# A macaron block (MoE, windowed top-k attention, MoE) on one core: an extra turn without a search, gates and value copies on ScalarE, two bias adds on GpSimd, a new interleaving

## The reference

```python
x = x + 0.5 * ffn(layernorm(x))      # layer zero
x = x + attn(layernorm(x))
x = x + 0.5 * ffn(layernorm(x))      # layer one, the same weights

def attn(x):                         # in windows of 128 tokens
    q, k, v = x @ Wq.T + bq, x @ Wk.T + bk, x @ Wv.T + bv
    scores = q @ k.T / sqrt(128)
    attn = softmax(scores where among the row's 32 largest, else -inf)
    out = leaky_relu(attn @ v, 0.01)
    return layernorm(out + x) * gamma + beta

def ffn(x):                          # 8 experts of width 384, the best 2 per token
    n = layernorm(x) * ln_gamma + ln_beta
    top_v, top_i = top_k(softmax(n @ router_w.T), 2)
    gates = softmax(top_v)
    return sum over the two of gate * swiglu_e(n) + swiglu_shared(n)
```

## Time and profile before

| | |
|---|---|
| median of 3 runs | 585.45 us (584.99 to 585.77) |
| span of the profiled execution | 581.5 us |
| TensorE busy | 500.6 us, 86% |
| VectorE busy | 388.7 us, 67% |
| GpSimd busy | 332.0 us, 57% |
| ScalarE busy | 330.0 us, 57% |
| mean granted TensorE clock | 0.951 |

### The profile page before, as it was taken

One profiled execution on the slowest core, in us unless ns is written; L12 is line 12 of the kernel. 1 busy time (PEld: TensorE's weight loads), 2 busy tenths in 40 slices (PEclk: granted clock), 3 DMA queues, 4 the chain that ended last, 5 costly groups with the idle time before them and its releaser, 6 DMA issues.

```text
span 581.5 us, 14497 instructions
## 1 busy us (share of the span) xinstructions
PE 500.6 (86%) x3928; PEld 458.6 (79%) x3928; DVE 388.7 (67%) x1688; ACT 330.0 (57%) x792; POOL 332.0 (57%) x491
## 2 busy tenths in 40 slices
PE   2588999989999989999977499996899999799781
PEld 1466999979899989998974369794889989799780
DVE  5558864732558989879887958999785624222574
ACT  3367556565467777667753357673655546555430
POOL 2273766875565675356674405664566765565542
PEclk9989999999999999999977569997999999999996
DMA  6944858766886554766412254431668767676993
GB/s 184 316 112 167 261 188 237 243 233 239 284 260 218 190 187 173 258 226 205 155 47 59 69 195 176 160 112 54 209 224 257 248 221 246 228 262 237 322 320 124
DMA packets 88012, 117.82 MB, mean 203 GB/s; under 512 B 11848, under 2 KB 60880, under 8 KB 87936
## 3 DMA queue, kind: packets, MB, share of 16 engines
q1 hardware_dynamic: 76208, 96.75, 49.8%
q0 software_dynamic: 9312, 19.16, 9.5%
q10 hardware_dynamic: 2416, 0.99, 0.7%
HBM read 26.57 MB, written 26.19 MB: 91 GB/s over the span
## 4 chain that ended last, share of the span: by engine, by line
PE 52%; SPq 15%; ACT 9%; DMA 7%; issue 7%; DVE 5%; POOL 3%; ACTq 1%; POOLq 0%; DVEq 0%
PE ps_y L730 12%; PE ps_g L716 11%; PE ps_u L721 6%; SPq L441 6%; PE ps_h L721 5%; DMA xin<-rows 5%; SPq L484 4%; SPq L479 3%; PE ps_x L711 2%; PE w L630 2%; SPq L499 2%; POOL rows L1572 2%; ACT zz L849 2%; PE w L660 2%; PE w L616 2%
## 5 line engine op out<-in xcount | busy, mean ns | idle before, releaser
L1589 POOL DMA_INDIRECT results<-raw_gu,idx x163 | 164.6, 1010 | 144.8 <-ACT raw_gu L929 103.1
L1572 POOL DMA_INDIRECT rows<-zz,s_idx x128 | 126.0, 984 | 66.9 <-issue 28.3
L730 PE MATMUL ps_y<-dn_t,raw_gu 128*128 x978 | 139.2, 279 | 5.7 <-ACT raw_gu L929 5.0
L716 PE MATMUL ps_g<-x_t,raw_dn 128*128 128x128 f32 x978 | 137.5, 277 | 0.0
L730 PEld LDWEIGHTS ps_y<-dn_t,raw_gu 128*128 128x128 f32 x978 | 123.4, 193 | 9.3 <-issue 8.5
L716 PEld LDWEIGHTS ps_g<-x_t,raw_dn 128*128 128x128 f32 x978 | 122.8, 192 | 3.6 <-issue 3.5
L929 ACT COPY raw_gu<-ps_y 128x128 f32<-128x128 f32 x163 | 42.9, 263 | 103.5 <-PE ps_y L730 101.8
L923 ACT ACTIVATE sil<-ps_g 128x384 f32<-128x384 f32 x163 | 80.1, 491 | 22.0 <-PE ps_g L716 20.8
L920 ACT ACTIVATE x_t<-ps_x,bf_c,gf_c 128x128 f32<-128x128 f32 x163 | 75.3, 462 | 19.6 <-PE ps_x L711 19.4
L1397 DVE TENSOR_TENSOR raw_gu<-sil,ps_u 128x384 f32<-128x384 f32 x82 | 44.9, 548 | 54.2 <-PE ps_u L721 47.2
L1397 DVE TENSOR_TENSOR raw_gu<-sil,ps_h 128x384 f32<-128x384 f32 x81 | 44.5, 550 | 50.8 <-PE ps_h L721 35.9
(11 more groups left out here) (172 smaller groups left out, 729.0 us busy)
## 6 DMA issues: line engine op xcount, KB each, us to landing
raw_dn<-gu_t SPq DMA_DIRECT2D x163, 384.0 KB
xin<-rows SPq DMA_DIRECT2D x163, 64.5 KB
yg<-results SPq DMA_DIRECT2D x15, 512.0 KB, 5.1
results<-raw_gu,idx POOLq DMA_INDIRECT x163
rows<-pads SPq DMA_DIRECT2D x40, 64.5 KB
rows<-pads SPq DMA_DIRECT2D x5, 451.5 KB
rows<-zz,s_idx POOLq DMA_INDIRECT x128, 2.4
out<-xres SPq DMA_DIRECT2D x7, 256.0 KB, 3.3
```

Of the source, the lines that this page charges most:

```text
L716: t = pe.matmul(ps_g[k][:, c, :], ws[:, k4, c * P:(c + 1) * P], x_t[:, k, :], start=True, stop=True)
L730: t = pe.matmul(ps_y[:, 0, :], h_t[:, k4, c * P:(c + 1) * P], dn[:, bass.ds(off + c * D, D)], start=(c == 0), stop=(c == FC - 1))
L1572: pool.indirect_dma_start(xs, bass.IndirectOffsetOnAxis(s_idx[n][:, c, k:k + 1], 0), zz[n][:, k, c, :], None).then_inc(scat[n], 16)
L1589: pool.indirect_dma_start(yt, bass.IndirectOffsetOnAxis(idx[:, ky:ky + 1], 0), yb[:, ky, :], None).then_inc(yst[ky], 16)
```

## The change

One constant gives one more turn, with no step searched, ahead of step 3: the turns become (0,-,-,1), (1,0,-,2), (2,1,0,-), **(-,2,1,-), (3,-,2,4), (4,3,-,5)**, (5,4,3,6) and on as before. For layer zero's results ScalarE multiplies `yg` by the gates in place, eight instructions of 128x128 per step (`gate`), and VectorE only adds (`add_gated`). ScalarE copies the values out of PSUM into `v` (new semaphore `v_cp`, for which PE now waits where the bank is used again), and GpSimd adds their bias (`values`, `v_sb`) and the attention's beta to the residual (`biased`), both in the turn of `a`. All five `WEAVE` lists are new.

```diff
-EMPTY_AT = ()
+EMPTY_AT = (3,)
...
 WEAVE = {
     "sp": """
-        8 7 3 8 2 2 13 8 24 12 4 45 9 13 12 1 48 9 7 z1 14 22 38 4 4 z1 1 z1 5 z1 3 z6""",
+        13 z2 21 2 6 1 3 27 4 21 35 7 5 25 6 2 61 6 1 7 14 42 4 z2 3 z1 6 3 z1 1 z5""",
...
@@ tensor
             def turn_p(A, done, keyed):
                 pe.wait_ge(pr_done, (A + 2) * TB)
+                pe.wait_ge(v_cp, A + 2)
...
             def keys(p, R, done):
-                pe.wait_ge(v_sb, p + 1)
+                pe.wait_ge(v_cp, p + 1)
...
             def shared_up(R, a, p):
-                    pe.wait_ge(v_sb, a + 2)
+                    pe.wait_ge(v_cp, a + 2)
...
@@ scalar
+            def values(a):
+                act.wait_ge(v_ps, a + 1)
+                act.copy(v[:], w1[:]).then_inc(v_cp, 1)
...
+            def gate(p):
+
+                act.wait_ge(gts, 1)
+                act.wait_ge(yld[p % 2], (p - p % 2) * 8 + 16)
+                for k in range(TB):
+                    for c in range(2):
+                        rows = yg[p % 2][:, k, c, :]
+                        act.activation(rows, rows, ACT.Copy, scale=gates[:, c, p * TB + k:p * TB + k + 1]).then_inc(gated, 1)
+                        turn()
...
                 if a in ALONE:
+                    gate(a)
                     norm_x(a, chain_alone[a])
...
                     keys(a)
                     turn()
+                    if p is not None:
+                        gate(p)
...
                     mix(A)
+                    turn()
+                if a is not None:
+                    values(a)
                     turn()
...
                 if a is not None:
                     exps(a)
+                if s + 1 < len(TURNS) and TURNS[s + 1].a not in ALONE and TURNS[s + 1].p is not None:
+                    gate(TURNS[s + 1].p)
...
@@ vector
+            def add_gated(p):
+
+                dve.wait_ge(gated, (p + 1) * 2 * TB)
+                xr = xres[:, p * TB:p * TB + TB, :]
+                for c in range(2):
+                    if c:
+                        dve.wait_ge(cb, p * N_CB + 2 * N_CB + 2)
+                    dve.tensor_tensor(xr, xr, yg[p % 2][:, :, c, :], ALU.add).then_inc(cb, 1 if c else 2)
+                    turn()
...
-            def biased(A):
-
-                dve.wait_ge(xn_done, A * TB + TB)
-                xr = xres[:, A * TB:A * TB + TB, :]
-                dve.tensor_tensor(xr, xr, wide(ba_b), ALU.add).then_inc(xb_done, 1)
-                turn()
...
-            def values(a):
-                dve.wait_ge(v_ps, a + 1)
-                dve.tensor_tensor(v[:], w1[:], bv_b[:].rearrange("p (o d) -> p o d", o=1).broadcast_to([P, TB, D]),
-                                  ALU.add).then_inc(v_sb, 1)
...
             def before(p):
 
-                combine(p, p % 2, p * TB)
+                add_gated(p)
                 stats_before(p, p * TB)
...
@@ gpsimd
+            def values(a):
+                pool.wait_ge(v_cp, a + 2)
+                pool.tensor_tensor(v[:], v[:], wide(bv_b), ALU.add).then_inc(v_sb, 1)
+
+            def biased(a):
+
+                pool.wait_ge(xn_done, a * TB + TB)
+                xr = xres[:, a * TB:a * TB + TB, :]
+                pool.tensor_tensor(xr, xr, wide(ba_b), ALU.add).then_inc(xb_done, 1)
...
+            pool.wait_ge(ld_c, 16 * 5)
             for a, A, J, *_ in TURNS:
+                if a is not None:
+                    values(a)
+                    turn()
+                    biased(a)
+                    turn()
                 if J is not None:
                     number(STEPS + J, J % RING, J * TB)
```

More of the change, by code:

```diff
@@ L119 @@
+        3 z1 18 1 z1 3 4 15 1 z3 2 7 z1 2 z1 1 4 16 1 z3 1 2 1 3 z3 2 5 z1 3 z1 3 4 7 2 z3 3 1 z1 6 z1 2 2 14 2 z1 9 1 1 2 19 5 2 5 1 25 2 1 3 z2""",
     "act": """
-        z12 1 1 z2 1 z1 2 3 z5 1 1 z4 1 6 3 1 z3 1 4 2 2 z4 5 2 z1 3 z3 9 4 2 11 5 56 2 z2 2 3 z1 3 7 z3 3 3 z4 1 4 2 z1 8 z2 1 2 3 1 z4 6 z1 4 4 z1
-        2 z1 2 4 3 z1 1 z2 21 z3 3 2 z1 2 2 z1 5 1 z6 2 z1 2 1 1 4 2 z3 5 2 3 3 z4 1 z2 1 z3 1 1 z15 1 z1 1 1 z1 2 z1 1 z2 8 z1 4 8 z8 1 2 z2 3 2 1
-        z2 4 z1 5 3 z6 3 z3 3 8 z4 2 3 3 15 1 z1 1 4 z1 3 40 15 1""",
+        z10 1 z1 2 1 2 z2 1 1 z4 1 z1 2 1 z1 1 z2 2 6 z1 4 z4 3 2 z1 1 z3 5 1 z1 2 z2 1 5 z1 1 14 9 41 z3 2 4 z2 9 z2 2 1 1 z3 1 z5 2 9 1 z1 1 z1 2
@@ L123 @@
+        1 z1 1 z4 1 z4 1 z3 4 1 2 z2 1 z1 2 z2 1 z2 8 z1 3 2 z2 1 z1 3 1 2 z2 1 z1 9 3 2 1 z1 1 1 4 1 z1 4 z6 8 2 z2 1 3 z9 4 1 8 z1 1 z7 3 z2 1 1
+        z1 1 1 z2 1 1 z1 1 z1 1 z3 10 2 2 1 z1 1 1 z15 1 2 z7 1 z3 1 z1 2 z3 1 z1 1 z4 1 z2 1 3 3 1 z1 1 1 1 z4 1 z1 1 2 1 1 z3 5 z1 1 6 3 z3 3 2 1
+        2 2 z2 4 z1 11 z1 1 z1 3 4 1 17 z2 2 5 1 z1 14 10 z1""",
     "dve": """
-        z153 1 z1 1 z4 1 z20 1 z11 1 z4 1 z5 1 z2 1 z9 1 z16 2 z7 2 z2 1 z9 2 z2 1 z13 1 z3 1 1 z1 1 z2 8 1 3 3 1 z2 1 z5 1 z4 1 z1 1 1 z3 1 z6 1 z5
@@ L125 @@
[L125 to L127 removed]
+        z133 1 z7 1 z5 1 z7 1 z14 1 z13 1 z8 1 z6 1 z17 1 z12 1 z5 1 z6 1 z1 1 z12 1 z5 1 z6 2 z4 1 z4 8 3 z1 7 z5 1 z2 1 z3 1 z2 2 1 z9 1 z4 1 z9 1
@@ L128 @@
+        z12 2 z10 1 z5 1 z9 1 z15 1 z11 1 z2 1 z9 1 z3 1 z18 1 z8 1 z7 1 z9 1 z8 1 z6 1 z9 1 z6 1 z6 1 1 z33 1 z7 1 1 z9 3 1 z9 1 z1 1 z10 1 z19 2
+        z2 1 z29 1 z1 1 z4 1 z4 1 z2 1 z7 1 1 z60 1 z11 1 z36 2 z15 1 z5 1 z8 1 z3 1 z12 1 z42 1 z7 1 z1 1 z4 1 z1 1 z17 1 z10 1 z4 1 z18 1 z9 1 z4
+        1 z8 1 z9 1 z2 1 z4 1 z19 1 z17 1 1 z13 1 z1 1 z5 1 z7 1 z2 1 z1 1 z30 1 z1 1 z2 1 z1 1 z7 1 z1 1 z4 26 z1 2 z4 1 1 1 z4 2 3 1 z2 2 z5""",
     "pool": """
-        z21 2 1 z1 1 z3 4 z2 3 z1 1 2 z1 5 1 2 2 1 1 3 1 2 z2 1 1 3 3 2 5 16 4 13 4 5 5 z1 5 1 1 2 2 z1 3 z2 2 5 31 z2 3 z1 5 4 z1 2 1 z1 5 1 z3 3
@@ L130 @@
-        z10 8 1 7 z1 2 1 1 1 2 2 z3 6 z4 3 z2 1 3 z1 5 5 1 4 2 2 2 z2 3 7 z3 10 7 1 10 3 3 10 40""",
+        z17 1 z2 1 1 1 z1 2 z4 3 1 z2 1 1 z3 3 1 3 2 1 z4 2 z1 1 1 5 1 1 1 2 z1 2 5 6 z1 17 z1 5 2 1 3 3 z2 14 z3 11 z1 4 12 z1 5 3 z1 3 4 z1 1 z1
+        11 1 z3 1 2 z3 2 1 z2 3 z1 4 z1 8 z4 4 z2 9 1 z5 2 2 z4 1 z1 5 z1 1 z1 10 1 z2 8 1 z1 5 z2 5 z1 1 5 z1 4 4 z1 1 z1 2 z1 7 6 z1 1 z1 1""",
 }
-VALUES, AFTER, AFTER_LATE, PICKS, SHARED, SHARED_LATE = 8, 13, 12, 19, 26, 31
+AFTER, AFTER_LATE, PICKS, SHARED, SHARED_LATE = 13, 12, 19, 26, 31
@@ L332, in macaron @@
             sem(n) for n in ("tl", "tl_e", "bl", "ended", "tab", "gts", "run0", "padded"))
-        cb = sem("cb")
+        cb, gated = sem("cb"), sem("gated")
         yld = [sem(f"yld{n}") for n in range(2)]
         yld_last = [[sem(f"yld_last{n}_{h}") for h in range(2)] for n in range(LAST_G)]
-        xn_done, xnT_ps, xnT_sb, q_ps, q_sb, k_ps, k_sb, v_ps, v_sb = (
-            sem(n) for n in ("xn_done", "xnT_ps", "xnT_sb", "q_ps", "q_sb", "k_ps", "k_sb", "v_ps", "v_sb"))
+        xn_done, xnT_ps, xnT_sb, q_ps, q_sb, k_ps, k_sb, v_ps, v_cp, v_sb = (
+            sem(n) for n in ("xn_done", "xnT_ps", "xnT_sb", "q_ps", "q_sb", "k_ps", "k_sb", "v_ps", "v_cp", "v_sb"))
         s_ps, sc_sb, tk, nm_done, ex_done, pr_done, ri_done, prT_ps, prT_sb, o_ps = (
@@ L356, in macaron @@
                    (y_ps, 8), (y_sb, 6), (shh, 1), (xr_done, 1), (prT_sb, 1), (pr_done, TB), (ex_done, TB),
-                   (nm_done, 1), (o_ps, 1), (o_sb, 1), (v_sb, 1), (x2_done, TB), (cb, 2 * 3)]
+                   (nm_done, 1), (o_ps, 1), (o_sb, 1), (v_sb, 1), (v_cp, 1), (x2_done, TB), (cb, 2 * 3)]
         ctx.enter_context(nc.allow_low_precision(reason="rows' numbers are whole and below 2**24, exact in float32"))
@@ L1484, in _ @@
                     stats_route(R, Jr, rt)
-                if A is not None:
-                    biased(A)
                 def between(m):
@@ L1491, in between @@
                         norms(m, chain_at[s], p, R)
-                    if m == VALUES and a is not None:
-                        values(a)
                     if m == after and A is not None:
@@ L1590, in slot, with wide @@
                                             yb[:, ky, :], None).then_inc(yst[ky], 16)
+            def wide(t):
+                return t[:].rearrange("p (o d) -> p o d", o=1).broadcast_to([P, TB, D])
+            def values(a):
[5 more added lines that the diff above has]
+                pool.tensor_tensor(xr, xr, wide(ba_b), ALU.add).then_inc(xb_done, 1)
             turn = Weave("pool", (0, 3), slot)
```

5 lines of the change are left out of this document (1 added, 4 removed).

## The result

The changed kernel takes 615.25 us (median of 4 runs, 610.65 to 623.41) against 585.22 (584.71 to 585.77) for the kernel before on the same chip: a ratio of 1.048, 95% interval 1.043 to 1.054. It is slower by some 28 to 30 us; the prediction said 571.0, faster, and its range ended at 586. The longest of the four runs fell into a slower state of the chip, and the ratio leaves it out. The profiled execution took 615.55 us, its span is 613.6.

What follows compares the result with a forecast made beforehand. TensorE was taken to bound 150 to 290 and 406 to 550 us, waits for lists the middle. Block 102 coming 14.4 us earlier cut the 581.5 span to 567.1; plus 3.95 gave 571.0 us, range 559 to 586.

Steps and rivals of the forecast that it cites:

- When does block 84 end? TensorE is the limit up to there: Layer zero's last blocks: block 84 ends at 307 us, bounds 301 and 312, against 310.06 before.
- Search 4 isn't in the way ... 295.5 at most: Search 4 on VectorE starts by 295.5 us at most (before 291.81) and ends by 316.5, before search 5 starts.
- step 3's data come some 5 us later: Ahead of search 4: the extra turn's products precede group 1's last blocks, delaying step 3's data some 5 us.
- turn 3 become 5.3 us shorter: VectorE's turn 3 drops `scaled` and `attended` (2.7 us) and a product, `values` and bias (2.6 us).
- search 5, gap, search 6: VectorE's middle: search 5 starts at 321.2 and takes 21.5 us, gap 8, search 6 20.1, ending at 370.8.
- Block 102 was to follow search 6 by 20.7: Second list's first block: follows search 6's end by 22.7 us minus 2, at 391.5, 14.4 us earlier.
- After it the same work remains: Behind block 102, where TensorE bounds: equal work remains, so the 14.4 us gain carries to the end.
- a step's eight in a row: ScalarE's gating: 0.33 us per product, 2.6 us per step (2.3 to 3.1); 2 us charged where not hidden.
- R3: Rival: in-order ScalarE gatings waiting for loads stop TensorE 2.6 us in each of eight runs; 590 us, slower; chance 0.16.
- The add was priced at 1.2 us: GpSimd's 16 adds of 128x512 take 1.2 us each, 19 us in all, between bounds of 0.675 and 2.3.
- Covered by its idle time: GpSimd's idle time (84.58 busy of 140 us) hides the adds' 19 us, as `v` is wanted a turn later.
- R4: Rival: twelve of 16 GpSimd adds each stop a VectorE chain instruction 1.2 us; 14.4 us, no change, 585.5; chance 0.07.

Runs made afterwards that it cites:

- sixth experiment: Changed kernel with layer zero's order up to the attention as in the kernel before, and both bias additions and the gates on VectorE: 587.58 us, ratio 1.005.
- fifth: Changed kernel with layer zero's order up to the attention as in the kernel before and both bias additions on VectorE, gates still on ScalarE: 590.55 us, ratio 1.011.
- the memsets: Changed kernel with GpSimd's 16 adds cut to one column of 128, each preceded by a GpSimd memset of 880 columns: 596.94 us, ratio 1.025.

## Why the prediction was wrong, point by point

**The step that failed first** is "When does block 84 end? TensorE is the limit up to there", 307 with bounds of 301 to 312. It priced what the extra turn pulls ahead and took the rest of the first 290 us as it was. In the changed kernel block 84 ended at 345.66. With layer zero's block work in the old order, and gates and adds on VectorE again, it ended at 309.37, inside the bounds. TensorE bounding that stage was rightly read; just because it does, a hole that a new order makes there delays all behind it: 144 instructions fewer by 150 us in the changed kernel, 125 fewer from 145 to 250 us in the sixth experiment. The new order, all five lists of it, had no term in the sum, and it and the adds are most of the loss: with layer zero's start and the adds undone the time is 590.55 instead of 615.25 us.

**The second**, for which the gain is missing too, is "Search 4 isn't in the way ... 295.5 at most". It measured 333.76, and 313.00 with the old order. The term "step 3's data come some 5 us later" was the wrong one. In the changed kernel the load of step 3's results is issued 36.9 us later, because block 61 ends at 268.6 instead of 230.8: the first step's holes again. With the old order it is 19.3 us later, by SyncE's list, while in VectorE's program the extra turn's own chain stands ahead of step 3 for 25 us, which the prediction hadn't counted. Nor did turn 3 become 5.3 us shorter: from search 3's start to search 4's there are 31.1 us in the changed kernel and 31.9 with the old order (where products and biases are VectorE's again, so that 2.7 of the 5.3 could show), 32.3 before.

**The steps behind it held.** Search 5, gap, search 6 were put at 21.5, 8 and 20.1 us; the run with the old order has 20.07, 7.41 and 20.28, the changed kernel 19.21, 6.62 and 22.64. Block 102 was to follow search 6 by 20.7; it followed by 21.30 in that run. From search 5 to block 102 that is 69.06 against 70.3: the chain was right, and its start was put 12.7 us too early. "After it the same work remains" was off by 4 us in that run (163.3 us from block 102 to the end of the last down product before, 167.6 there) and by 7 in the changed kernel (170.4); why layer one's new order takes longer stays open.

**ScalarE.** A gate product lasted 0.39 us by itself and 0.33 us of busy time, as priced; a step's eight in a row took 2.4 to 2.9 us, 2.6 as forecast. R3 (ScalarE holds up TensorE) did not come: undoing the gates changes nothing that can be measured in the changed kernel, and about 3 us with the old start (fifth against sixth experiment), where the intervals just part. Put into the kernel before, the gates cost 27 us, but not by the wait that the prediction named, a gate that stands for its load with the blocks behind it: there VectorE stands for gates that come late in ScalarE's list, and TensorE for VectorE.

**GpSimd.** The add was priced at 1.2 us and took 1.28 to 1.33 in the mean. "Covered by its idle time" was right of its queue, as the memsets show, and wrong of VectorE. R4 was the true mechanism of a third to a half of the loss. It was sized at 14.4 us, near the 11 to 14 measured, in part by luck (twelve stops of 1.2 us on the path, where there are eleven of 0.5 to 3.0 us); it had 0.07, because "most adds fall within a search, whose instructions read one tile". The search is interleaved with two-input instructions, and in five of eight steps one add follows the other at once, so that in four of them one VectorE instruction waits for both, 2.7 to 3.0 us.
The Trainium skill's "SBUF — State Buffer" (Who interferes with whom) says that a VectorE instruction with two SBUF inputs and a GpSimd instruction that reads SBUF exclude each other, and one with a single SBUF input, outside the modes that use both pairs of ports, is free. The trace agrees: all eleven stretched instructions have two SBUF inputs, and beside the add at 248.73 a `MATCH_REPLACE8` keeps its 0.28 us.

What stays open: which places of the new order from 145 to 250 us lose the block work (only the whole was undone), and which of the stretched instructions lie on the path, since 18.8 us of stretch cost 11 to 14, and the 6.9 us that the memsets stretched VectorE by (below) cost nothing that can be told; and what the extra turn gives with step 3's load issued early and layer one in the old order.

## What to carry to other kernels

An order planned anew is a change of its own: before pricing the moved instructions, count how much of the bounding engine's work stands ahead of each step in the old list and in the new one. In a stage that one engine bounds, work moved away from another engine bought nothing here, and a hole costs up to its full length: block 30's 19 us brought 20 back, block 84's last 16 us only 1, since another chain ended later. When a step is pulled forward, look at the queue that issues its load too, not only at the engine that computes it. Before work goes to GpSimd, look at which VectorE instructions will run beside it, not at GpSimd's idle time.

## What the runs showed of the hardware

Two adjacent GpSimd adds can hold one VectorE instruction for their whole sum: 0.33 us became 3.19, 0.69 became 3.66. It is held until the second add ends (352.16 and 352.00), and seems to be held from before the first add's recorded start: the 0.33 us from 348.97 would have been over before 349.51. A memset on GpSimd, which reads nothing, leaves two-input adds alone (two of 128x512 beside the first memset took 0.69 and 0.73 us, 0.69 elsewhere) but holds another form. VectorE's and GpSimd's timelines of that run:

```profile
239.82 1.37 DVE L1104 TENSOR_SCALAR var_e<-mv 128x4 f32<-128x4 f32 x1
239.89 1.30 DVE L1390 MAX8 top<-wk_s 128x8 f32<-128x128 f32 x1
```

```profile
240.32 0.85 POOL L1624 MEMSET scr<- 128x880 f32 x1
```

A `TENSOR_SCALAR` of 4 columns, usually 0.17 us, lasts until the memset ends, and the `MAX8` behind it in VectorE's queue seems to last as long. Eight instructions beside three memsets were stretched so, by 6.9 us in all.
By the same page of the Trainium skill (Who interferes with whom) a `tensor_scalar` can enter a mode in which VectorE uses both pairs of ports; the trace agrees with it, though no row names the mode.
